# A two-layer graph network: tiles of gathered rows by matrix products instead of indirect transfers, and smaller products on parts of the array

## The reference, cut to what matters

```
h  = relu(layernorm(x))
x  = x + relu( segsum(w * (h @ W0 + b0)[src], dst) / (segsum(w, dst) + 1e-6) )      # layer one
h  = relu(layernorm(x))
m  = gelu( concat(h[src], edge_attr) @ W_msg + b_msg )                              # per edge
x  = x + gelu( ((1 + eps) * h + segsum(m, dst)) @ W_upd + b_upd )                   # layer two
```

## Time and profile before

| what | value |
|---|---|
| median of 3 runs | 3535.41 us (3535.20 to 3536.32) |
| the profiled execution's own time | 3536.93 us |
| its span, first to last instruction | 3535.1 us |
| busy: TensorE / VectorE / ScalarE / GpSimd | 82% / 61% / 55% / 73% |
[...]

### The profile page before, as it was taken

The page is one execution under the profiler, slowest core; times in us unless marked ns, Lnnn a source line. Parts: engine busy times, 40 slices in busy tenths (PEclk is TensorE's granted clock), DMA queues, the critical chain, the costliest instruction groups (busy, mean ns, idle before and its releaser), DMA issues.

```text
span 3535.1 us, 89327 instructions
## 1 busy us (share of the span) xinstructions
PE 2887.9 (82%) x31003; PEld 2758.6 (78%) x31004; DVE 2160.5 (61%) x3525; ACT 1944.3 (55%) x6492; POOL 2570.7 (73%) x2720
## 2 busy tenths in 40 slices
PE   1988888887888888888778888888888888888887
PEld 1987877877877777778777878787787878787877
DVE  5766666666666666666655555556565655565653
ACT  3655565655555656555565555555454555555553
POOL 4777777777777777777457777777777777777774
PEclk9999999999899899999678989898988899898988
DMA  3322222222222222222123333333333333333331
GB/s 97 60 48 53 50 48 50 50 52 50 48 53 50 48 50 50 52 50 48 32 63 74 75 73 77 74 81 72 76 74 74 74 74 74 74 74 74 74 74 48
DMA packets 277341, 220.23 MB, mean 62 GB/s; under 512 B 81018, under 2 KB 208518, under 8 KB 277314
## 3 DMA queue, kind: packets, MB, share of 16 engines
q0 software_dynamic: 86240, 88.48, 16.6%
q1 hardware_dynamic: 191074, 131.40, 13.1%
HBM read 214.39 MB, written 5.30 MB: 62 GB/s over the span
## 4 chain that ended last, share of the span: by engine, by line
POOL 71%; issue 24%; SPq 2%; PE 1%; POOLq 1%; DMA 1%; ACT 1%; DVE 0%; DVEq 0%
POOL rows L436 71%; PE ps L719 1%; SPq L307 1%; SPq L328 0%; POOLq L434 0%; ACT sums_sb L566 0%; DMA h_table<-h_sb 0%; POOLq L427 0%; SPq L300 0%; DMA p_table<-h_sb 0%; PE ps L745 0%; PE ps L679 0%; DMA rows<-h_table,idx 0%; SPq L304 0%; DVE h_sb L834 0%
## 5 line engine op out<-in xcount | busy, mean ns | idle before, releaser
L647 PE MATMUL ps<-parts,pick_all 125*128 125x192 bf16 x19600 | 1767.9, 253 | 54.6 <-DVE pick_all L930 30.8
L930 DVE TENSOR_SCALAR pick_all<-src_bc,node_f 125x1280 bf16<-125x1280 int16 (+1 forms) x1960 | 1740.0, 953 | 71.1 <-issue 52.7
L647 PEld LDWEIGHTS ps<-parts,pick_all 125*128 125x128 bf16 x19600 | 1692.6, 101 | 87.5 <-issue 57.1
L436 POOL DMA_INDIRECT rows<-p_table,idx x1372 | 1295.6, 944 | 440.0 <-issue 440.0
L436 POOL DMA_INDIRECT rows<-h_table,idx x1323 | 1248.6, 944 | 415.9 <-issue 415.9
L511 ACT ACTIVATE onehot<-iota,dw 128x72 f32<-128x72 f32 x3136 | 809.3, 342 | 0.0
L679 PE MATMUL ps<-onehot,room 128*65 128x72 f32 (+1 forms) x6272 | 546.4, 248 | 268.9 <-ACT room L541 262.5
L679 PEld LDWEIGHTS ps<-onehot,room 128*65 128x65 f32 (+1 forms) x6272 | 488.4, 155 | 328.1 <-ACT room L541 293.5
L586 ACT ACTIVATE room<-room 128x512 f32<-128x512 f32 x196 | 123.6, 630 | 783.9 <-DVE room L1095 783.3
L1095 DVE TENSOR_TENSOR room<-ps,rows 128x512 f32<-128x512 f32 x196 | 135.5, 691 | 618.0 <-DMA rows<-p_table,idx 600.7
L769 PE MATMUL ps<-W1b_sb,eT 128*128 128x128 f32 x1568 | 259.7, 318 | 252.1 <-ACT eT L581 251.9
(11 more groups left out here) (87 smaller groups left out, 567.2 us busy)
## 6 DMA issues: line engine op xcount, KB each, us to landing
src_bc<-last_src SPq DMA_DIRECT2D x196, 312.5 KB
ea<-in_edge_attr_dram SPq DMA_DIRECT2D x196, 256.0 KB, 5.4
rows<-p_table,idx POOLq DMA_INDIRECT x1372
rows<-h_table,idx POOLq DMA_INDIRECT x1323
src_bc<-last_src SPq DMA_DIRECT2D x49, 156.2 KB
x_sb<-in_x_dram SPq DMA_DIRECT2D x5, 312.5 KB
h_table<-h_sb SPq DMA_DIRECT2D x5, 312.5 KB
p_table<-h_sb SPq DMA_DIRECT2D x5, 312.5 KB
```

Source lines behind the costliest of these rows:

```text
L436: nc.gpsimd.indirect_dma_start(out=rows[:, s, j, 0:D], out_offset=None, in_=table[:, :], in_offset=bass.IndirectOffsetOnAxis(ap=idx[:, s, ...
L647: last = nc.tensor.matmul(psG[(s + shift) % 2], pick[layer][(s + shift) // 2 % 2][0:PN, n, at:at + P], parts[:, n, :], start=(n == 0), sto ...
L930: last = nc.vector.tensor_scalar(pick[layer][i][0:PN, c * KN:(c + 1) * KN, :], src_bc[:, i, :, 0:w], node_f[:, c:c + 1], None, ALU.is_equal)
```

## The change

For layer and pair, `EXTRA` says whether TensorE also fetches tile 6 of the odd group: both pairs of a body in layer one, the first of two in layer two. Its 50 products are cut in two halves around the gathers (`next_gathers`); the compare matrices and the source broadcasts of those pairs become 384 wide. The edge product is cut into eight products on 64 rows of the array each, into two PSUM banks (5 and 6), and moves behind the windows of the group before it. In layer two the eight window products go in turn to array columns (PSUM partitions) 0 to 63 and 64 to 127, the sums are kept in two halves, and `Wu_sb` holds `W_upd` twice so that the last product adds them; its bias is now added by VectorE ahead of gelu. The target and weight tables are separate, the target as int16, so ScalarE copies two pieces per group in layer one.

```diff
@@ -81,8 +81,9 @@
     JG = J - 1
-    EXTRA = 2
-    JP = [[JG - (layer == 0 and s == EXTRA) for s in range(SLOTS)] for layer in range(2)]
+    EXTRA = ((1, 1), (1, 0))
+    JP = [[JG - (s % 2 == 1 and EXTRA[layer][s // 2]) for s in range(SLOTS)] for layer in range(2)]
@@ -131,9 +133,9 @@
         src_bc = sb("src_bc", [PN, 2, KN, PE3 + 16], i16)
-        pick_all = sb("pick_all", [P, NK * (PE3 + PE2)], bf16)
-        pick = [[pick_all[:, 0:NK * w].rearrange("p (n e) -> p n e", n=NK),
-                 pick_all[:, NK * PE3:NK * (PE3 + PE2)].rearrange("p (n e) -> p n e", n=NK)] for w in (PE3, PE2)]
+        pick_all = sb("pick_all", [P, 2 * NK * PE3], bf16)
+        pick = [[pick_all[:, i * NK * PE3:i * NK * PE3 + NK * (PE3 if EXTRA[layer][i] else PE2)].rearrange(
+            "p (n e) -> p n e", n=NK) for i in range(2)] for layer in range(2)]
@@ -187,7 +191,7 @@
         psT = ps[:, 1, :]
-        psM = ps[:, 2, :]
+        psM = [ps[:, 5 + h, 0:J // 2 * D] for h in range(2)]
@@ -195,7 +199,7 @@
         psG = [ps[:, 3 + i, 0:SPLIT * D] for i in range(2)]
-        psX = ps[:, 5, 0:SPLIT * D]
+        psX = ps[:, 2, 0:SPLIT * D]
@@ -266,11 +268,19 @@
         s_fin_mm = sem("update_multiplied")
+        s_fin_b = sem("update_bias_added")
...
         block = ctx.enter_context(nc.Block())
+        def width(layer, i):
+            return PE3 if EXTRA[layer][i] else PE2
+        def extras(layer, b, i):
+            return b * sum(EXTRA[layer]) + sum(EXTRA[layer][0:i + 1])
@@ -316,9 +326,9 @@
                 sp.dma_start(src_bc[:, i, :, 0:PE2], v.to_broadcast([PN, KN, PE2])).then_inc(s_bc[layer][i], 16)
-                if layer == 0 and i == 0:
-                    v = last_src[0].rearrange("k g e -> k (g e)")[:, bass.ds((q + EXTRA // 2) * PE2, P)].rearrange(
+                if EXTRA[layer][i]:
+                    v = last_src[0].rearrange("k g e -> k (g e)")[:, bass.ds(q * PE2 + P, P)].rearrange(
@@ -343,8 +353,9 @@
                 sp.dma_start(W1b_sb[h * D:(h + 1) * D, h * D:(h + 1) * D], W_msg[D:2 * D, :]).then_inc(s_w, 16)
-            sp.dma_start(Wu_sb[0:D, :], W_upd).then_inc(s_w, 16)
-            sp.dma_start(Wu_sb[D:DA, :], b_upd.rearrange("(a n) -> a n", a=1)).then_inc(s_w, 16)
+            for h in range(2):
+                sp.dma_start(Wu_sb[h * D:(h + 1) * D, :], W_upd).then_inc(s_w, 16)
+            sp.dma_start(bu_bc[:, :], b_upd.rearrange("(a n) -> a n", a=1).to_broadcast([PN, D])).then_inc(s_w, 16)
@@ -422,7 +433,7 @@
                     pool.wait_ge(s_agg, UNITS)
-                    nc.gpsimd.memset(sums_sb[D:DA, :], 1.0).then_inc(s_ones, 1)
+                    nc.gpsimd.memset(sums_sb[D:DA, :], 0.0).then_inc(s_cleared, 1)
@@ -442,8 +453,9 @@
-                nc.scalar.copy(dw[:, slot, :, :].rearrange("p q j -> p (q j)"),
-                               dw_tab[:, bass.ds(g, 1), :, :].rearrange("p a q j -> p (a q j)")).then_inc(s_dw[layer], 1)
+                if layer == 0:
+                    nc.scalar.copy(dw[:, slot, 1, :], w_tab[:, bass.ds(g * J, J)])
+                nc.scalar.copy(dw[:, slot, 0, :], dst_tab[:, bass.ds(g * J, J)]).then_inc(s_dw[layer], 1)
@@ -535,8 +547,8 @@
                     act.wait_ge(s_prow[0], g + 2)
-                    if s == EXTRA:
-                        act.wait_ge(s_xrow, b + 1)
+                    if s % 2 and EXTRA[0][s // 2]:
+                        act.wait_ge(s_xrow[0], extras(0, b, s // 2))
@@ -595,8 +607,8 @@
             for c in range(NC):
-                act.wait_ge(s_fin_mm, c + 1)
-                nc.scalar.activation(h_sb[:, c, :], psN[c % 2][0:PN, 0:KN * D], ACT.Gelu_apprx_tanh).then_inc(s_fin_g, 1)
+                act.wait_ge(s_fin_b, c + 1)
+                nc.scalar.activation(h_sb[:, c, :], h_sb[:, c, :], ACT.Gelu_apprx_tanh).then_inc(s_fin_g, 1)
@@ -648,36 +660,38 @@
-            def extra(q):
-                for n in range(q * NK // 4, (q + 1) * NK // 4):
-                    last = nc.tensor.matmul(psX, pick[0][0][0:PN, n, PE2:PE3], parts[:, n, :],
+            def extra(layer, i, half):
+                for n in range(half * NK // 2, (half + 1) * NK // 2):
+                    last = nc.tensor.matmul(psX, pick[layer][i][0:PN, n, PE2:PE3], parts[:, n, :],
...
-            def next_extra(b, s, last_body):
-                if s == 0:
-                    extra(2)
-                elif s == 1:
-                    extra(3).then_inc(s_xpicked, 1)
-                elif s == 2 and not last_body:
-                    pe.wait_ge(s_half, b + 1)
-                    pe.wait_ge(s_xrow, b + 1)
-                    extra(0)
-                elif s == 3 and not last_body:
-                    extra(1).then_inc(s_xused, 1)
-            def windows(layer, b, s, lhs, width):
+            def next_gathers(layer, b, s):
+                i = (s + 1) // 2 % 2
+                if s % 2:
+                    gather(layer, b, s, 1)
+                    if EXTRA[layer][i]:
+                        pe.wait_ge(s_xrow[layer], extras(layer, b + (s + 1) // SLOTS, i) - 1)
+                        extra(layer, i, 0)
+                else:
+                    if EXTRA[layer][i]:
+                        extra(layer, i, 1).then_inc(s_xpicked[layer], 1)
+                    gather(layer, b, s, 1)
+            def windows(layer, b, s, lhs, width, sets):
...
                     for j in range(J):
-                        last = nc.tensor.matmul(psW[s % 2][0:width, :], lhs(j), onehot[:, s % 2, j, :],
-                                                start=(j == 0), stop=(j == J - 1))
+                        at = j % sets * width
+                        last = nc.tensor.matmul(psW[s % 2][at:at + width, :], lhs(j), onehot[:, s % 2, j, :],
+                                                start=(j < sets), stop=(j >= J - sets))
@@ -692,17 +706,16 @@
             gather(0, 0, 0, 0)
-            extra(0)
-            extra(1).then_inc(s_xused, 1)
+            if EXTRA[0][0]:
+                extra(0, 0, 0)
...
                     if not (last_body and s == SLOTS - 1):
-                        gather(0, b, s, 1)
-                    next_extra(b, s, last_body)
+                        next_gathers(0, b, s)
                     pe.wait_ge(s_used[s], b + 2)
-                    windows(0, b, s, lambda j, s=s: wrows[:, s % 2, j, :], DA)
+                    windows(0, b, s, lambda j, s=s: wrows[:, s % 2, j, :], DA, 1)
@@ -765,25 +778,31 @@
                     pe.wait_ge(s_used[s], b + (1 + BODIES + 1))
                 for q in range(J // 2):
-                    last = nc.tensor.matmul(psM[:, q * P:(q + 1) * P], eT[:, q * P:(q + 1) * P],
-                                            W1b_sb[:, :], start=True, stop=True)
+                    for h in range(2):
+                        last = nc.tensor.matmul(psM[h][:, q * D:(q + 1) * D],
+                                                eT[h * D:(h + 1) * D, q * P:(q + 1) * P],
+                                                W1b_sb[h * D:(h + 1) * D, h * D:(h + 1) * D], start=True, stop=True)
...
             gather(1, 0, 0, 0)
+            if EXTRA[1][0]:
+                extra(1, 0, 0)
...
                         edge_transpose(b, s, 1)
-                        gather(1, b, s, 1)
+                        next_gathers(1, b, s)
+                    pe.wait_ge(s_msg, b * SLOTS + (s + 1 + 2))
+                    windows(1, b, s, lambda j, s=s: msg[:, s % 2, j * D:(j + 1) * D], D, 2)
+                    if not (last_body and s == SLOTS - 1):
                         edge_product(b, s, 1)
-                    pe.wait_ge(s_msg, b * SLOTS + (s + 1 + 2))
-                    windows(1, b, s, lambda j, s=s: msg[:, s % 2, j * D:(j + 1) * D], D)
@@ -791,11 +810,10 @@
             pe.wait_ge(s_done, 2 * NG + 2)
-            pe.wait_ge(s_ones, 1)
...
                 if c >= 2:
-                    pe.wait_ge(s_fin_g, c - 1)
+                    pe.wait_ge(s_fin_b, c - 1)
@@ -940,12 +955,8 @@
                     dve.wait_ge(s_pick[layer], 2 * b + (s + 3) // 2)
-                    if layer == 0 and s == 1:
-                        dve.wait_ge(s_xused, b + 1)
                     sources(layer, (s + 3) // 2 % 2, b + ((s + 3) // 4 + 1))
-                    last = pick_half(layer, (s + 3) // 2 % 2, 0)
-                    if layer == 0 and s == 1:
-                        last.then_inc(s_half, 1)
+                    pick_half(layer, (s + 3) // 2 % 2, 0)
@@ -962,11 +973,11 @@
-            def extra_rows(b):
-                dve.wait_ge(s_xpicked, b + 1)
-                nc.vector.tensor_reduce(rows[:, EXTRA, JG - 1, 0:D], psX.rearrange("p (q d) -> p d q", q=SPLIT),
-                                        AX.X, ALU.add).then_inc(s_xrow, 1)
+            def extra_rows(layer, b, s):
+                dve.wait_ge(s_xpicked[layer], extras(layer, b, s // 2))
+                nc.vector.tensor_reduce(rows[:, s + 1, JG - 1, 0:D], psX.rearrange("p (q d) -> p d q", q=SPLIT),
```

(70 more changed lines are left out.)

## The result

The changed kernel takes 3412.82 us (median of 4 runs, 3412.45 to 3414.27) where the one before takes 3535.6: a ratio of 0.9651, 95% interval 0.9638 to 0.9664. The forecast was 3413.5 us. The profiled execution took 3412.54 us, its span is 3410.7 us.

The account below looks back on a forecast made before the run. GpSimd's own issue rate was taken to bound both layers. From the profiled 3536.93 us, 122.4 for removed transfers went off and 0.5 for the end came on: 3415.0, or 3413.5 us as median (execution 1.5 above median); range 3408 to 3440.

Parts of the forecast that it names:

- TensorE, layer one: Gather, half tile and windows take 7.25 us per group, 29.0 per body, covered by GpSimd's 32.46 at mean clock above 0.89.
- rival D: TensorE's clock falls to 0.88 in layer one, a body of 33.0 us, 24 given back, 3438 us; chance 6%.
- TensorE, layer two: Transposes, gathers, half tiles, edge product and windows take 28.4 us per body, covered by GpSimd's 33.72.
- I take two rows of loads side by side, 8 x 0.108 = 0.87, and 0.58: Layer two, per group: edge product 0.87 us with row halves overlapping, windows halved to 0.58, together 1.45 us.
- The 0.108 us: Time per weight load at full clock, from the last product's 0.217 us at clock 0.50, used for layer two's edge product.
- Three changes at 0.16 us: Layer two: switching the array's division empties it, 0.5 us per group, bringing 1.45 to 1.95, still covered.
- rival C: Layer two: tile changes and small products take 3.67 us per group, body 37.26, 173 us given back, 3587 us; chance 5%.
- B: Array parts don't overlap: layer two's edge product and windows take 2.88 us, body 34.1, 3433 us; chance 11%.
- E: Something called covered is not, such as a late broadcast or a release, and eats the whole gain; chance 2%.
- Covered work: Start costs nothing, stretch between layers is covered, end takes 0.5 us more; edges together between -3 and +4 us.
- GpSimd's share of the chain: Sign of a right forecast: GpSimd still holds about 71% of the chain that ended last.
- a step of TensorE over 8.4 us in layer two: Sign of a wrong forecast: any TensorE step in layer two longer than 8.4 us.

Follow-up runs that it names:

- u2_l2_none: Changed kernel with no additional tile fetched by TensorE in layer two, 49 indirect transfers more: 3474.76 us.
- u5_skip_one: Changed kernel with the fetch of tile 6 in slot 3 of layer two left out and nothing put in its place: 3350.97 us.
- u4_l2_both_hoist: Changed kernel with the additional tile for both pairs of layer two and TensorE's window-count load ahead of its wait in both layers: 3424.79 us.
- v2_both_hoist_full: Changed kernel with the additional tile for both layer-two pairs, the early register load, and full-width edge and window products: 3501.14 us.
- u3_l2_both: Changed kernel with the additional tile for both pairs of layer two, 49 transfers fewer: 3526.15 us.
- v3_both_hoist_edgefull: Changed kernel with the additional tile for both layer-two pairs, early register load, full-width edge product: 5711.94 us where the kernel before took 5286.05.

## Why the prediction was right

**The bound and the saving.** 98 transfers at 1.2485 and 1.249 us were to save 122.4 us; the two layers shrank by 121.6 and the median by 122.8. Taking and giving transfers one per body (`u2_l2_none`, `u5_skip_one`) gave 61.9 us both ways, and 61.4 and 61.0 against kernels on the same chip, beside 61.2 worked out. The step that carried the forecast was reading idle time that ends with "issue" as an issue rate and not as slack.

**TensorE, layer one.** The forecast had 7.25 us per group, 29.0 per body, under GpSimd's 32.46: it stayed under, with GpSimd waiting 0.3 us in the whole layer. The clock rose from 0.93 to 0.98, as argued; rival D is out.

**TensorE, layer two.** The conclusion (covered) held, the term did not. I took 1.45 us for windows and edge product, bounds 1.08 and 2.88; they take 2.2 to 2.3 per group in the changed kernel. The step that failed is "I take two rows of loads side by side, 8 x 0.108 = 0.87, and 0.58". That the edge product's loads go side by side in two rows was my assumption, and no run shows it; in place of the 0.87 us its sixteen loads took 0.97 in `u4_l2_both_hoist`, and the product 1.04. The windows did nearly halve (0.65 us to the next product, once nothing stands between, against 1.14 in `v2_both_hoist_full`): 1.69 together. The larger part of the miss is a term that the sum did not have at all: the register load behind the windows, about 0.5 us, which had been hidden by the very products that the change shortens (loading early gives 5 us with full-width windows and 101 with narrow ones). The body came to 31.7 us by the rows of `u3_l2_both`, not 28.4; the margin to 33.72 was 2 us, not 5. That the missed load still fitted into the margin was luck: nothing in the forecast had made room for it. The 0.108 us itself came from a row that I described wrongly. Its "65*125" is 65 rows of the array by 125 columns of weights, with 64 columns of data, and it was scaled from a stretch at clock 0.50; the sixteen instructions of the edge product's eight products, on 64 rows, take 0.065 us each.

**Changes of the array's division.** Three changes at 0.16 us stood in the price of rival C. In `u4_l2_both_hoist` sixteen window loads take 0.57 us and the edge product, on another division, starts 0.65 us after the first of them; sixteen loads of the edge product take 0.97, and the transposes start 1.04 us after the first of those. Nothing like 0.16 us per change is seen at these two: from the end of the loads to the next product there are 0.08 and 0.07 us, and 0.07 also in `v2_both_hoist_full`, from the windows' loads to the edge product, both in full width. At the third, from a gather to the windows in column halves, the windows start 4.21 to 4.22 us after the gather, and in full width, in that run, they start 4.22 after it. That the array empties at a change was my assumption, and no run shows it. In column halves eight window products go in 0.65 us, in full width in 1.14. Whether the row halves work side by side stays open: they take no less than four full products (1.04 against 0.99), but also less than the 1.73 us at which the forecast put eight such products without overlap, and no run had them on one half alone.

**Rivals.** B needs 2.88 us for edge product and windows; the two took 2.2 to 2.3, and 1.69 without the register load, so its price is out, although the edge product gained nothing over four full products. C needs 3.41 us. `u3_l2_both` shows what C would have looked like: one more tile per body, and TensorE's 36.0 us give back 113 us. Of E nothing was seen: GpSimd's idle time ends with "issue" but for 0.3 us.

**Covered work.** The start and the stretch between the layers, costed at nothing, changed by -1.4 and -1.0 us. The end was to gain 0.5 us and changed by -0.4: the bias addition is on the path with 0.50 us, but the last windows, now in column halves, take 1.25 us where they took 2.19. These pieces outweigh the 0.8 us by which the layers fell short of 122.4, and the profiled execution shrank by 124.4 us and not by the 121.9 of the sum. The median came within 0.7 us of the forecast in part because the profiled execution before lay 1.5 us above its median and the one after 0.3 below; so close a hit is luck, the size of the saving is not.

**Signs named in advance.** Two went the other way. GpSimd's share of the chain is 35% instead of 71, for the reason given above. And a step of TensorE over 8.4 us in layer two was to show the forecast wrong: a group with a half tile takes 8.99. That sign was badly put, since 8.4 us is a quarter of GpSimd's 33.72 and only the sum of the four groups of a body counts; the group without a half tile takes 7.15.

## What to carry to other kernels

Idle time of an engine that ended with "issue" at a constant interval (1.25 us from one of GpSimd's transfers to the next) was that engine's own rate here; count its instructions first, and cost everything else only to see whether it stays below. Before shortening products on an engine that branches, look for register loads and other work of its sequencer that the long products hide: here half a microsecond appeared that cost more than the shorter products gave. And a part of a change that makes room should be tried alone, for here the room was there without it.

## What was not expected of the hardware

A register load of TensorE from SBUF, between two groups of products, left the engine idle for 0.42 to 0.51 us in the rows shown, and moving it ahead of a semaphore wait took all of it away (101 us over 196 groups). Eight fp32 products of 64x128 weights on two row halves take 1.04 us, about as long as four of 128x128 with twice the data (0.99 us); eight products in two column halves take 0.65 us instead of 1.14. And two of the four chips of the experiments ran the kernel before in 5286 and 5270 us instead of 3536. On them the changed kernel with the early load was 9% slower than the kernel before (ratios 1.0897 and 1.0928), with gaps of 0.4 to 1.5 us between TensorE's products in the rows shown; the changed kernel itself was not run there. It has 6,468 more loads and as many more products than the kernel before, but `v3_both_hoist_edgefull`, with 882 more again, was faster there. What makes these chips slow, and why these kernels lose there, stays open.
